# Graph-attention layers with the sources on the partitions and seven groups of destination blocks

## The chip, the cores and the metric

One core of one Trainium2 chip runs the whole program. The metric is the device time of one execution in microseconds. The kernel before took 3711.85 us (median of three runs, 3707.11 to 3715.58).

## The reference

The input is a graph of 3125 nodes with 256 features, 100,000 directed edges and a loop at each node (103,125 edges). Four stages follow, each added to its own input after a layer norm: graph attention with 8 heads of 32 channels, a feed-forward with 16 experts of which each row uses 2, three single-head attention layers with gelu, and a feed-forward on the rows that a router picks. The change is about the third stage, and what prepares it:

```python
def gat_conv(x, src, dst, W, a_src, a_dst, b):
    h = x @ W
    s = h @ a_src
    d = h @ a_dst
    alpha = jax.nn.leaky_relu(s[src] + d[dst], NEG_SLOPE)
    m = jax.ops.segment_max(alpha, dst, num_segments=n)
    ex = jnp.exp(alpha - m[dst])
    denom = jax.ops.segment_sum(ex, dst, num_segments=n)
    w = ex / (denom[dst] + 1e-16)
    out = jax.ops.segment_sum(h[src] * w[:, None], dst, num_segments=n)
    return out + b
x = jax.nn.gelu(gat_conv(x, src, dst, W1, as1, ad1, b1), approximate=False)
```

It is applied three times with other weights; the heads stage is the same with 8 heads and without gelu.

## The kernel before

The edges become a dense matrix `mask_dram` of 3125 x 3200 floats: minus the logarithm of the number of edges, or a large number where there is none. Attention is then dense: for each destination, over all 3125 sources. Nodes stand in 25 blocks of 128 (the last has 53).

The program is a row of phases: edges and nodes to 84 us, the matrix to 450, the heads to 1834, routed nodes and experts to 2308, node projections to 2366, the three layers to 3517, the last feed-forward to 3707. Every engine has its own hand-written list of instructions; waits on semaphores are all that orders one against another.

**Heads** (`heads_phase`). Two passes of four heads over 25 blocks, 200 units in all; a unit is one head of one block, destinations on the partitions. DVE computes the 3125 scores (L977), adds the mask and takes the minimum of the negated scores (`maxima`, L981). ACT exponentiates in two halves (`exps`, L914) and sums as it goes. PE transposes the probabilities in four groups of 7, 6, 6 and 6 tiles into two banks `psT` (L1013), ACT copies each to SBUF (`copy_out`, L923), and PE multiplies (L1027) into one of three banks `psO`. Once a block ACT copies the sums (`copy_sums`, L929), PE turns them (L1034) and ACT writes the rows in four scaled pieces (`rows`, L938). POOL adds the two halves of the denominators (L886) and stores the rows; SP loads the masks, 1568 KB a block.

**Projections** (`node_project_phase`) make for each node the features times W with two more columns, and spread one of them over all partitions as `el` in two versions (times 1 and times the slope).

**Layers** (`layers_phase`). The same scheme as in the heads with one head of 256 channels and 25 blocks a layer:

- DVE: `maxima` (L1308, L1312, L1316) two blocks ahead; `sums` and `rows` (L1342 to L1361); the copies of what the next layer needs: `copy_x` (L1368), `copy_h` (L1373), `copy_el` (L1380, L1381).
- ACT: `exps` (L1486), `copy_out` (L1495), `gelu` (L1500), between which its function table is loaded again.
- PE: `transposes` of the probabilities (L1535), `products` (L1546), then for the next layer `transpose_x` (L1556), `project` (L1565) and `spread_el` (L1573).
- SP: one mask load a block (L1287).

A layer can't start before the last block of the one before is projected and spread; `first_maxima` makes the first block's maxima in two parts for that reason (L1326, L1330). In the last layer DVE also adds the stage's input, normalises and sums for the router, and PE turns the result back (L1582, copied at L1421).

## Time and profile before

| | |
|---|---|
| median of three runs | 3711.85 us |
| profiled execution, its own time | 3708.9 us |
| span of its trace | 3707.2 us |
| granted TensorE clock, mean | 0.973 |
| PE, DVE, ACT, POOL busy | 3419.1, 2806.4, 2514.1, 317.8 us |
| HBM read, written | 327.87, 61.11 MB |

The span is one profiled execution from its first to its last instruction; 1.7 us lie around it. A busy time is the sum of an engine's instructions in it. PE is TensorE's matmuls and PEld its weight loads, which run beside them; DVE is VectorE, ACT ScalarE, POOL GpSimd, SP SyncE. In the records a transpose counts once and a product twice. The mean of the busy shares hides that the stages have different limits.

### The profile page before, as it was taken

How to read it: one execution, taken by the hardware profiler on the slowest of the kernel's cores; microseconds unless marked ns; L12 is line 12 of the kernel's file. 1: busy time of each engine (PE TensorE's matmuls, PEld its weight loads, DVE VectorE, ACT ScalarE, POOL GpSimd, SP SyncE). 2: the span in 40 equal slices, each digit the busy share in tenths (PEclk: the TensorE clock that was granted, in tenths of full speed). 3: DMA queues.
4: the chain of work that ended last, by engine and by line, in shares of the span. 5: the costliest groups of instructions: out<-in, count | busy, mean ns of one | idle time of the engine just before them, and what ended most of it. 6: DMA issues, size and time to landing. Idle time of an engine off the chain costs nothing. (4 is left out here: it accounts for less than half of the span.)

```text
span 3707.2 us, 69969 instructions
## 1 busy us (share of the span) xinstructions
PE 3419.1 (92%) x27369; PEld 2683.0 (72%) x27370; DVE 2806.4 (76%) x4237; ACT 2514.1 (68%) x4068; POOL 317.8 (9%) x280
## 2 busy tenths in 40 slices
PE   6999889999999999999769998799999999999999
PEld 4665566666666666666568998688878888888777
DVE  6999999999999999999762222666655565677594
ACT  4999899999999999999711111466656665676532
POOL 1000011001000010010004444000000000000000
PEclk8999999999999999999859999899999999999999
DMA  4433312122124121121158885422223221433101
GB/s 144 173 109 140 130 57 74 56 63 67 56 69 190 56 74 56 63 66 56 51 180 269 234 242 121 142 105 105 105 86 115 105 105 62 175 115 112 37 15 35
DMA packets 144871, 390.36 MB, mean 105 GB/s; under 512 B 20048, under 2 KB 91550, under 8 KB 126750
## 3 DMA queue, kind: packets, MB, share of 16 engines
q1 hardware_dynamic: 120520, 346.56, 26.7%
q0 software_dynamic: 20816, 36.07, 5.0%
q8 instruction: 224, 3.67, 0.4%
q10 hardware_dynamic: 3206, 3.20, 0.4%
q14 instruction: 105, 0.86, 0.1%
HBM read 327.87 MB, written 61.11 MB: 105 GB/s over the span
## 5 line engine op out<-in xcount | busy, mean ns | idle before, releaser
L923 ACT ACTIVATE hd_probsT<-hd_psT 128x768 f32<-128x768 f32 (+1 forms) x800 | 659.9, 852 | 70.5 <-PE hd_psT L1013 70.5
L1027 PE MATMUL hd_psO<-hd_probsT,hx 128*32 128x128 f32 (+1 forms) x10000 | 571.8, 281 | 129.1 <-ACT hd_probsT L923 129.0
L1546 PE MATMUL ly_psO<-hx_a,ly_probsT 128*128 128x256 f32 x2500 | 584.1, 381 | 0.0
L1027 PEld LDWEIGHTS hd_psO<-hd_probsT,hx 128*32 128x32 f32 (+1 forms) x10000 | 317.3, 108 | 322.5 <-ACT hd_probsT L923 216.0
L1495 ACT ACTIVATE ly_probsT<-ly_psT 128x768 f32<-128x768 f32 (+1 forms) x300 | 248.4, 828 | 392.7 <-PE ly_psT L1535 392.5
L1546 PEld LDWEIGHTS ly_psO<-hx_a,ly_probsT 128*128 128x128 f32 x2500 | 454.1, 190 | 71.4 <-issue 16.6
L1013 PE MATMUL hd_psT<-ident,hd_scores 128*128 128x128 f32 (+1 forms) x3325 | 479.0, 281 | 0.0
L977 DVE SCALAR_TENSOR_TENSOR hd_scores<-el_heads,hx 128x3125 f32<-128x3125 f32 x133 | 460.8, 3465 | 0.0
L981 DVE CUSTOM_DVE_ANT_0 hd_scores<-hd_scores,mask_heads 128x3125 f32<-128x3125 f32 x133 | 453.6, 3411 | 5.7
L914 ACT ACTIVATE hd_scores<-hd_scores,negmax 128x1664 f32<-128x1664 f32 (+1 forms) x266 | 429.9, 1616 | 5.6 <-DVE negmax L981 5.6
L1013 PEld LDWEIGHTS hd_psT<-ident,hd_scores 128*128 128x128 f32 (+1 forms) x3325 | 355.6, 141 | 98.9 <-issue 98.9
L1546 PE MATMUL ly_psO<-hx_b,ly_probsT 128*128 128x256 f32 x1250 | 292.0, 381 | 0.0
L488 DVE TENSOR_SCALAR onehot_c<-iotaC,stage_c 128x392 bf16<-128x392 f16 x1176 | 291.5, 326 | 0.0
L1535 PE MATMUL ly_psT<-ident,ly_scores 128*128 128x128 f32 x1875 | 258.0, 276 | 16.6 <-ACT ly_scores L1486 16.6
L2007 ACT ACTIVATE moe_hidden<-moe_ps_h 128x512 f32<-128x512 f32 x64 | 38.2, 597 | 327.1 <-PE moe_ps_h L1972 327.1
L1486 ACT ACTIVATE ly_scores<-ly_scores,ly_negmax 128x1664 f32<-128x1664 f32 (+1 forms) x150 | 239.3, 1595 | 20.7 <-DVE ly_negmax L1312 10.0
L1546 PEld LDWEIGHTS ly_psO<-hx_b,ly_probsT 128*128 128x128 f32 x1250 | 226.9, 189 | 35.6 <-issue 8.3
L1013 PE MATMUL hd_psT<-ident,scores 128*128 128x128 f32 (+1 forms) x1675 | 243.1, 283 | 9.0 <-ACT scores L914 9.0
L1312 DVE CUSTOM_DVE_ANT_0 ly_scores<-ly_scores,ly_mask 128x3125 f32<-128x3125 f32 x73 | 248.9, 3410 | 3.1
L1535 PEld LDWEIGHTS ly_psT<-ident,ly_scores 128*128 128x128 f32 x1875 | 220.9, 142 | 40.4 <-ACT ly_scores L1486 17.1
L1972 PEld LDWEIGHTS moe_ps_h<-moe_xT,moe_w 128*128 128x128 f32 x2048 | 241.5, 194 | 5.5 <-DVE moe_xT L2013 2.2
L1972 PE MATMUL moe_ps_h<-moe_xT,moe_w 128*128 128x128 f32 x2048 | 242.0, 277 | 1.6 <-DVE moe_xT L2013 1.6
(348 smaller groups left out, 5041.0 us busy)
## 6 DMA issues: line engine op xcount, KB each, us to landing
ly_mask<-mask_dram SPq DMA_DIRECT2D x72, 1568.0 KB, 6.6
moe_w<-in_L_ffn_w SPq DMA_DIRECT2D x144, 512.0 KB, 5.0
mask_heads<-mask_dram SPq DMA_DIRECT2D x46, 1568.0 KB, 6.7
mask_dram<-el_heads SPq DMA_DIRECT2D x196, 196.0 KB, 1.9
el_heads<-el_dram SPq DMA_DIRECT2D x5, 1568.0 KB, 9.7
el_heads<-el_slope_dram SPq DMA_DIRECT2D x5, 1568.0 KB, 13.1
x<-x SPq DMA_DIRECT2D x8, 640.0 KB, 8.4
el_heads<-el_dram POOLq DMA_DIRECT2D x3, 1568.0 KB
```

The lines of the kernel that those rows point to most:

```text
L488: last = nc.vector.tensor_scalar(oc[:, k, :], g["iotaC"][:, :], c[:, k:k + 1], None, ALU.is_equal)
L914: nc.scalar.activation(sc[u % 3][:, halves[j]], sc[u % 3][:, halves[j]], ACT.Exp, scale=-1.0, bias=nm[:, u % 3:u % 3 + 1], accum_out=den[: ...
L923: nc.scalar.activation(pT[:, gi % 2, 0:w], psT[gi % 2][:, 0:w], ACT.Copy).then_inc(s_ev, 1)
L977: nc.vector.scalar_tensor_tensor(sc[c][:, :], el[:, h, 0, 0:N], hx[:, b, o:o + 1], el[:, h, 1, 0:N], ALU.subtract, ALU.min).then_inc(s_lk, 1)
L981: nc.vector.tensor_tensor_reduce(out=sc[c][:, :], in0=sc[c][:, :], in1=mask[:, B % 2, 0:N], scale=1.0, scalar=3.0e38, op0=ALU.add, op1=ALU ...
L1013: last = nc.tensor.transpose(psT[gi % 2][0:r, t * P:(t + 1) * P], sc[u % 3][:, c0:c0 + r], g["ident"][:, :])
L1027: last = nc.tensor.matmul(psO[B % 3][cg * CH:(cg + 1) * CH, h * P:(h + 1) * P], hx[0:r, tt, c0:c0 + CH], pT[0:r, gi % 2, t * P:(t + 1) * P ...
L1312: nc.vector.tensor_tensor_reduce(out=sc[:, c, :], in0=sc[:, c, :], in1=mask[:, B % 2, 0:N], scale=1.0, scalar=3.0e38, op0=ALU.add, op1=ALU ...
L1495: nc.scalar.activation(pT[:, gi % 2, 0:w], psT[gi % 2][:, 0:w], ACT.Copy).then_inc(s_ev, 1)
L1535: last = nc.tensor.transpose(psT[gi % 2][0:r, t * P:(t + 1) * P], sc[:, B % 3, c0:c0 + r], g["ident"][:, :])
L1546: last = nc.tensor.matmul(psO[B % 2][:, 0:D], pT[0:r, gi % 2, t * P:(t + 1) * P], hx[B // NB % 2][0:r, tt, 0:D], start=tt == 0, stop=tt == ...
L1972: last = nc.tensor.matmul(out[:, m * P:(m + 1) * P], w12[:, t % WS, i, k, m * P:(m + 1) * P], xT[:, t % 2, k, :], start=k == 0, stop=k == 1)
```

## The change

The three layers are turned round: sources stand on the partitions and destinations in the free dimension, so that DVE's scores are already the left operand of the product, and no transposes of probabilities or copies of them are left.

- Destination blocks go in seven groups of 3, 3, 4, 5, 5, 3 and 2. A group has 13 steps of two source tiles; scores, exponentials and mask pieces stand in a ring of four steps. Each block of a group has a PSUM bank of its own, with 257 columns: column 0 of the table is ones, so its product is the denominator.
- The scores need each destination's shift along the free dimension. DVE makes the maxima as before (custom operation of 3125 columns, without the score operation ahead of it) for the blocks of the next group, at the steps named in `at_step`, computes two numbers a destination from them (`shifts`), PE spreads these over the partitions (`spread_rows`) and ACT copies them (`copy_rows`).
- The sums of a group are copied out of PSUM one block at a time by ACT (`drain`) after the exponentials of the next group's step 1; `rows` on DVE and `gelus` on ACT follow at step 3.
- `copy_x`, `copy_h` and `copy_el` go from DVE to ACT; the last layer's additions go to POOL, its normalisation to ACT.
- The next layer's first three maxima are made in three pieces of 2560, 384 and 181 columns and joined (`maxima_part`, `maxima_joined`); those of layer 0 in four pieces in the projection phase, which loads three masks now.
- The turned mask `maskT_dram` is made in the heads: PE transposes 3 or 4 tiles of the block's mask a unit into a bank of its own (`turn_mask`, `psM`; `psO` has two banks then), ACT copies them (`copy_mask`) and SP stores them (`store_turned`). The router phase writes the changed diagonal into both matrices.
- In the heads ACT copies the rows in one piece, and POOL multiplies them by the reciprocals.

The core of the diff (left out: the declarations, the projection phase, the pieces of the maxima, the last layer's own operations and the loops of SP and POOL):

```diff
-        psO = [ctx.enter_context(nc.psum_tensor(f"hd_psO{i}", [P, 512], F32)) for i in range(3)]
+        psO = [ctx.enter_context(nc.psum_tensor(f"hd_psO{i}", [P, 512], F32)) for i in range(2)]
+        psM = ctx.enter_context(nc.psum_tensor("hd_psM", [P, 512], F32))
+        mt = sb("mask_turned", [P, 2, HG * P])
...
+            def store_turned(j):
+                b, r, ks = j // HG % NB, dest(j), chunk(j)
+                sp.wait_ge(s_mc, j + 1)
+                whole = [k for k in ks if k < FULL]
+                sp.dma_start(g["maskT_dram"][whole[0] * P:(whole[-1] + 1) * P, b * P:b * P + r].rearrange("(k p) d -> p k d", p=P),
+                             mt[:, j % 2, 0:len(whole) * P].rearrange("p (k d) -> p k d", d=P)[:, :, 0:r]).then_inc(s_mst[j % 2], 16)
...
                 if B + 1 < BLOCKS:
                     halves_added(B + 1)
+                pool.wait_ge(s_raw, B + 1)
+                pool.wait_ge(s_rd, B + 1)
+                rows_ = y[:, B % 3, :].rearrange("p (h c) -> p h c", c=CH)
+                nc.gpsimd.tensor_tensor(rows_, rows_, rden[:, B % 3, :].rearrange("p (h o) -> p h o", o=1).broadcast_to([P, HG, CH]),
+                                        ALU.mult).then_inc(s_y, 1)
...
                     act.wait_ge(s_store[i], 16 * (B // 3))
-                for h in range(HG):
-                    last = nc.scalar.activation(y[:, i, h * CH:(h + 1) * CH], psY[:, h * CH:(h + 1) * CH], ACT.Copy,
-                                                scale=rden[:, i, h:h + 1])
-                last.then_inc(s_y, 1)
+                nc.scalar.activation(y[:, i, :], psY[:, 0:P], ACT.Copy).then_inc(s_raw, 1)
+            def copy_mask(j):
+                act.wait_ge(s_mT, j + 1)
+                if j >= 2:
+                    act.wait_ge(s_mst[j % 2], stored_upto(j - 2))
+                w = len(chunk(j)) * P
+                nc.scalar.activation(mt[:, j % 2, 0:w], psM[:, 0:w], ACT.Copy).then_inc(s_mc, 1)
...
+                    if gi == 3 and u + 2 < UNITS:
+                        copy_mask(u + 2)
...
+            def turn_mask(j):
+                B = j // HG
+                r = dest(j)
+                if B >= 2:
+                    pe.wait_ge(s_mask[B % 2], 16 * (B // 2))
+                if j:
+                    pe.wait_ge(s_mc, j)
+                for t, k in enumerate(chunk(j)):
+                    m = min(P, N - k * P)
+                    last = nc.tensor.transpose(psM[0:m, t * P:t * P + r], mask[0:r, B % 2, k * P:k * P + m], g["ident"][0:r, 0:r])
+                last.then_inc(s_mT, 1)
...
+SIZES = (3, 3, 4, 5, 5, 3, 2)
...
+KC = 2
+NCK = -(-NB // KC)
+RING = 4
...
+        at_step = {5: (0, 1, 2, 3, 5), 4: (0, 1, 3, 5), 3: (0, 2, 4), 2: (1, 3)}
+        first_steps = (2, 4, 6)
+        assert SIZES[1] == len(first_steps)
+        shift_step = lambda G: 7 if G % NG == 1 else 5
...
+        turn_at = {}
+        for gi in range(NG - 1):
+            for i in range(SIZES[gi]):
+                turn_at[STARTS[gi] + i] = (gi + 1) * NCK + 4 + (i if gi + 1 == NG - 1 else 2 * i)
...
+            def load_turned(C):
+                G, c = C // NCK, C % NCK
+                c0, w, s = STARTS[G % NG] * P, width(G), C % RING
+                if C >= RING:
+                    sp.wait_ge(s_msk, C - RING + 1)
+                ks = tiles(c)
+                r = depth(ks[-1])
+                sp.dma_start(mT[0:r, s, 0:len(ks), 0:w],
+                             g["maskT_dram"][ks[0] * P:ks[0] * P + len(ks) * r, c0:c0 + w].rearrange("(k p) d -> p k d", p=r)).then_inc(s_mT[s], 16)
...
+                    nc.gpsimd.tensor_tensor(x[:, b, :], x[:, b, :], y_last[:, b, :], ALU.add).then_inc(s_add, 1)
...
+            def scores(C):
+                G, c = C // NCK, C % NCK
+                l, w, s = G // NG, width(G), C % RING
+                if C >= RING:
+                    multiplied(dve, C - RING)
...
+                for i, k in enumerate(tiles(c)):
+                    r = depth(k)
+                    last = nc.vector.scalar_tensor_tensor(pb[0:r, s, i, 0:w], rw[0:r, G % 2, 0, 0:w], hx[l % 2][0:r, k, N8:N8 + 1],
+                                                          rw[0:r, G % 2, 1, 0:w], ALU.add, ALU.min)
+                last.then_inc(s_lk, 1)
+            def masked(C):
+                G, c = C // NCK, C % NCK
+                w, s = width(G), C % RING
+                n, r = len(tiles(c)), depth(tiles(c)[-1])
+                dve.wait_ge(s_lk, C + 1)
+                dve.wait_ge(s_mT[s], 16 * (C // RING) + 16)
+                nc.vector.tensor_tensor(pb[0:r, s, 0:n, 0:w], pb[0:r, s, 0:n, 0:w], mT[0:r, s, 0:n, 0:w], ALU.add).then_inc(s_msk, 1)
...
+                nc.vector.tensor_tensor_reduce(out=m[:, 0:N], in0=el[B // NB % 2][:, 0:N], in1=m[:, 0:N], scale=1.0, scalar=3.0e38,
+                                               op0=ALU.add, op1=ALU.min, accum_out=q[:, G % 2, d:d + 1]).then_inc(s_nm, 1)
...
+            def rows(G):
+                l, n = G // NG, size(G)
+                dve.wait_ge(s_dr, first_of(G) + n)
...
+                for gi in range(NG):
+                    G = G0 + gi
+                    for c in range(NCK):
+                        C = G * NCK + c
+                        scores(C)
+                        if gi or c:
+                            masked(C - 1)
+                        if gi + 1 < NG:
+                            for d in range(size(G + 1)):
+                                if maxima_at[first_of(G + 1) + d] == C:
+                                    maxima(first_of(G + 1) + d, G + 1)
+                            if c == shift_step(G + 1):
+                                shifts(G + 1)
+                        elif l < LAST and c in (4, 6, 8):
+                            maxima_part(l + 1, 0, (c - 4) // 2)
+                        if gi and c == 3:
+                            rows(G - 1)
+                        if l == LAST and gi:
...
+            def exps(C):
+                G, c = C // NCK, C % NCK
+                l, w, s = G // NG, width(G), C % RING
+                act.wait_ge(s_msk, C + 1)
+                for i, k in enumerate(tiles(c)):
+                    r = depth(k)
+                    last = nc.scalar.activation(pb[0:r, s, i, 0:w], pb[0:r, s, i, 0:w], ACT.Exp, scale=-1.0,
+                                                bias=hx[l % 2][0:r, k, B2:B2 + 1])
+                last.then_inc(s_ex, 1)
...
+            def drain(G):
+                if G:
+                    done = first_of(G)
+                    act.wait_ge(s_y, done)
+                    if (G - 1) // NG < LAST:
+                        act.wait_ge(s_xT, done)
+                for d in range(size(G)):
+                    act.wait_ge(s_done, first_of(G) + d + 1)
+                    nc.scalar.activation(ob[:, d, :], psO[d][:, 0:D + 1], ACT.Copy).then_inc(s_dr, 1)
...
+                    for c in range(NCK):
+                        t = gi * NCK + c
+                        exps(G * NCK + c)
+                        if gi and c == 1:
+                            drain(G - 1)
+                        if gi and c == 3:
+                            gelus(G - 1)
+                        if gi + 1 < NG and c - shift_step(G + 1) in range(1, 1 + 2 * SPREADS[gi + 1], 2):
+                            copy_rows(G + 1, (c - shift_step(G + 1)) // 2)
+                        if l < LAST:
+                            for b in due(t - 1):
+                                copy_x(l * NB + b)
...
+            def products(C):
+                G, c = C // NCK, C % NCK
+                l, w, s = G // NG, width(G), C % RING
+                pe.wait_ge(s_ex, C + 1)
+                for i, k in enumerate(tiles(c)):
+                    r = depth(k)
+                    for d in range(size(G)):
+                        if k == 0 and G and d < size(G - 1):
+                            pe.wait_ge(s_dr, first_of(G - 1) + d + 1)
+                        m = min(P, w - d * P)
+                        last = nc.tensor.matmul(psO[d][0:m, 0:D + 1], pb[0:r, s, i, d * P:d * P + m], hx[l % 2][0:r, k, 0:D + 1],
+                                                start=k == 0, stop=k == NB - 1)
+                        if k == NB - 1:
+                            last.then_inc(s_done, 1)
+                if c < NCK - 1:
+                    last.then_inc(s_mm, 1)
...
+                    for c in range(NCK):
+                        t = gi * NCK + c
+                        products(G * NCK + c)
+                        if gi + 1 < NG and c - shift_step(G + 1) in range(0, 2 * SPREADS[gi + 1], 2):
+                            spread_rows(G + 1, (c - shift_step(G + 1)) // 2)
+                        if l < LAST:
+                            for b in due(t - 1):
+                                project(l * NB + b)
+                            for b in due(t):
+                                transpose_x(l * NB + b)
+                            for b in due(t - 2):
+                                spread_el(l * NB + b)
```

How the rows of each engine move. First ACT in the heads, around the write of a block's rows (`hd_y_stage`); `scores` and `hd_scores` are the three score buffers. Before:

```order
L923 ACTIVATE hd_probsT<-hd_psT 128x768
L938 ACTIVATE hd_y_stage<-hd_psY,hd_rden 128x32 x4
L923 ACTIVATE hd_probsT<-hd_psT 128x768
L914 ACTIVATE hd_scores,hd_den<-hd_scores,negmax 128x1461
L923 ACTIVATE hd_probsT<-hd_psT 128x896
L923 ACTIVATE hd_probsT<-hd_psT 128x768
L914 ACTIVATE scores,hd_den<-scores,negmax 128x1664
```

And now:

```order
L959 ACTIVATE hd_probsT<-hd_psT 128x768
L972 ACTIVATE hd_y_stage<-hd_psY 128x128
L959 ACTIVATE hd_probsT<-hd_psT 128x768
L979 ACTIVATE hd_mask_turned<-hd_psM 128x384
L950 ACTIVATE hd_scores,hd_den<-hd_scores,negmax 128x1461
L959 ACTIVATE hd_probsT<-hd_psT 128x896
L959 ACTIVATE hd_probsT<-hd_psT 128x768
L950 ACTIVATE hd_scores,hd_den<-hd_scores,negmax 128x1664
```

The four writes of 32 columns are one of 128, and a copy of the turned mask stands ahead of the second half of the exponentials of the next unit.

Second DVE in the layers. Before, a steady block:

```order
L1308 SCALAR_TENSOR_TENSOR ly_scores<-el,hx_a 128x3125
L1311 MEMSET ly_spare 1x1
L1312 ISA ly_scores,ly_negmax<-ly_scores,ly_mask 128x3125
L1312 ISA ly_negmax 128x1
L1316 TENSOR_SCALAR ly_has_edge<-ly_negmax 128x1
L1380 COPY x<-ly_psX 128x128
L1381 TENSOR_SCALAR x<-ly_psX 128x128
L1368 COPY ly_xT<-ly_psX 128x256
L1342 TENSOR_TENSOR ly_rden<-ly_den 128x1
L1344 RECIPROCAL ly_rden<-ly_rden 128x1
```

Now, from the last step of group 0 to the start of group 1 (three blocks each; L1493 are the scores, L1503 the mask, L1510 a maximum for group 2):

```order
L1493 SCALAR_TENSOR_TENSOR ly_probs<-ly_rows,hx_a 128x384 x2
L1503 TENSOR_TENSOR ly_probs<-ly_probs,ly_mask_turned 53x384
L1510 ISA ly_mask,least<-el,ly_mask 128x3125
L1510 ISA least 128x1
L1493 SCALAR_TENSOR_TENSOR ly_probs<-ly_rows,hx_a 128x384 x2
L1503 TENSOR_TENSOR ly_probs<-ly_probs,ly_mask_turned 128x2x384
L1510 ISA ly_mask,least<-el,ly_mask 128x3125
L1510 ISA least 128x1
L1493 SCALAR_TENSOR_TENSOR ly_probs<-ly_rows,hx_a 128x384 x2
L1503 TENSOR_TENSOR ly_probs<-ly_probs,ly_mask_turned 128x2x384
L1493 SCALAR_TENSOR_TENSOR ly_probs<-ly_rows,hx_a 128x384 x2
L1503 TENSOR_TENSOR ly_probs<-ly_probs,ly_mask_turned 128x2x384
```

One pair of long operations a block has become 13 steps of scores and mask a group, with the maxima of the next group between the first of them.

Third ACT at the same place (L1638 exponentials, L1650 the drain of group 0, L1656 its gelu):

```order
L1638 ACTIVATE ly_probs<-ly_probs,hx_a 53x384
L1638 ACTIVATE ly_probs<-ly_probs,hx_a 128x384 x4
L1650 ACTIVATE ly_sums<-ly_psO 128x257 x3
L1638 ACTIVATE ly_probs<-ly_probs,hx_a 128x384 x4
L1656 ACT_TABLE_LOAD
L1656 ACTIVATE ly_sums<-ly_sums 128x256 x3
L1638 ACT_TABLE_LOAD
L1638 ACTIVATE ly_probs<-ly_probs,hx_a 128x384 x4
```

The drain stands behind the exponentials of steps 0 and 1 of the new group, and the gelu behind those of steps 2 and 3. Before, no such drain existed: DVE read the sums from PSUM at L1361.

## Rows read from the trace of the kernel before

**Rows 1.** Busy us by stretch: PE, PEld, DVE, ACT, POOL; clock, DMA share, GB/s.
```profile
450.00:1834.00 1384.00, 1245.97 (x15400) 893.80 (x15400) 1359.74 (x849) 1298.71 (x1855) 129.42 (x105) 1.00 0.22 70
2366.00:3517.00 1151.00, 1124.32 (x6075) 959.82 (x6075) 712.68 (x1099) 711.02 (x835) 0.00 (x0) 0.99 0.29 104
```

**Rows 2.** Costliest groups, shapes apart, 2366 to 3517 us: busy, mean ns | idle before.
```profile
L1546 PE MATMUL ly_psO<-hx_a,ly_probsT 128*128 128x256 f32 x2400 | 552.8, 379 | 0.0
...
L1312 DVE CUSTOM_DVE_ANT_0 ly_scores<-ly_scores,ly_mask 128x3125 f32<-128x3125 f32 x73 | 248.9, 3410 | 3.1
...
L1308 DVE SCALAR_TENSOR_TENSOR ly_scores<-el,hx_a 128x3125 f32<-128x3125 f32 x49 | 169.8, 3465 | 3.9 <-DMA ly_mask<-mask_dram 2.2 <-PEq L59 1.7
L1486 ACT ACTIVATE ly_scores<-ly_scores,ly_negmax 128x1664 f32<-128x1664 f32 x75 | 125.7, 1676 | 19.9 <-DVE ly_negmax L1312 10.0 <-DVE ly_negmax L1335 9.9
...
L1486 ACT ACT_TABLE_LOAD x76 | 97.5, 1283 | 2.1 <-PEq L59 0.8
```

**Rows 3.** Timeline of a steady block of a layer, PE alone: start us, length us.
```profile
2600.45 0.38 PE L1556 MATMUL ly_psX<-ident,ly_y 128*128 128x128 f32 x2
...
2600.67 0.93 PE L1535 MATMUL ly_psT<-ident,ly_scores 128*128 128x128 f32 x7
...
2601.43 2.95 PE L1546 MATMUL ly_psO<-hx_a,ly_probsT 128*128 128x256 f32 x12
...
2604.31 1.14 PE L1565 MATMUL ly_psH<-wx,ly_xT 128*128 128x258 f32 x4
...
2605.94 3.19 PE L1546 MATMUL ly_psO<-hx_a,ly_probsT 128*128 128x256 f32 x14
...
2608.97 0.27 PE L1573 MATMUL ly_psX<-ident,hx_b 128*128 128x128 f32 x1
```

**Rows 4.** Timeline: first products of layers 0 and 1, first record after the last.
```profile
2377.82 1.59 PE L1546 MATMUL ly_psO<-hx_a,ly_probsT 128*128 128x256 f32 x3
...
2767.88 2.42 PE L1546 MATMUL ly_psO<-hx_b,ly_probsT 128*128 128x256 f32 x7
...
3507.43 0.44 PE L1582 MATMUL ly_psH<-ident,hx_b 128*128 128x128 f32 x2
```

**Rows 5.** Timeline of the boundary between layers 0 and 1.
```profile
2758.06 0.29 DVE L1380 COPY x<-ly_psX 128x128 f32<-128x128 f32 x1 [0.58 <-PE ly_psX L1573]
2758.27 0.28 DVE L1381 TENSOR_SCALAR x<-ly_psX 128x128 f32<-128x128 f32 x1
...
2762.20 0.41 DVE L1326 SCALAR_TENSOR_TENSOR ly_scores<-x,hx_b 128x181 f32<-128x181 f32 x1
...
2765.05 3.04 PE L1535 MATMUL ly_psT<-ident,ly_scores 128*128 128x128 f32 x13 [3.28 <-ACT ly_scores L1486]
```

**Rows 6.** Timeline of the heads: maxima of two units, two copies.
```profile
998.91 3.41 DVE L981 CUSTOM_DVE_ANT_0 hd_scores<-hd_scores,mask_heads 128x3125 f32<-128x3125 f32 x1
...
1004.08 1.50 ACT L923 ACTIVATE hd_probsT<-hd_psT 128x768 f32<-128x768 f32 x2
...
1005.76 3.41 DVE L981 CUSTOM_DVE_ANT_0 scores<-scores,mask_heads 128x3125 f32<-128x3125 f32 x1
```

**Rows 7.** Waits in the heads, 500 to 1800 us: total us, times, longest.
```profile
PE hd_psO L1027 <- ACT hd_probsT L923: 122.6, 238, 1.7
...
ACT hd_probsT L923 <- PE hd_psT L1013: 64.9, 141, 0.7
```

**Rows 8.** Costliest groups of the heads, shapes apart, 500 to 1800 us.
```profile
L923 ACT ACTIVATE hd_probsT<-hd_psT 128x768 f32<-128x768 f32 x568 | 454.6, 823 | 64.9 <-PE hd_psT L1013 64.9
...
L938 ACT ACTIVATE hd_y_stage<-hd_psY,hd_rden 128x32 f32<-128x32 f32 x188 | 38.6, 300 | 0.0
...
L929 ACT ACTIVATE hd_sumsT<-hd_psO 128x512 f32<-128x512 f32 x47 | 27.6, 587 | 0.0
```

**Rows 9.** The tile of the denominators in the heads: least, median and longest ns.
```profile
L886 POOL TENSOR_TENSOR hd_rden<-hd_den x50: 191/1710/3443, 478.5 to 1824.4; 128x4 f32<-128x4 f32 x50
```

**Rows 10.** The page's DMA issues: KB each, us from issue to landing.
```profile
ly_mask<-mask_dram SPq DMA_DIRECT2D x72, 1568.0 KB, 6.6
```

More of the change, by code:

```diff
@@ new lines, in layers_phase @@
+        depth = lambda k: min(P, N - k * P)
+        spreads_upto = lambda G: G // NG * sum(SPREADS) + sum(SPREADS[:G % NG])
+        place, user, landed = {}, {}, {}
+        latest, loads = [None] * len(masks), [0] * len(masks)
+        for B in range(LAYERS * NB):
+            if B < 2:
+                s = B
+            elif B % NB == SIZES[0] - 1:
+                s = 2
+            else:
+                s = 0 if latest[1] > latest[0] else 1
+            place[B], user[B] = s, latest[s]
+            latest[s] = B
+            loads[s] += 0 if B < SIZES[0] else 1
+            landed[B] = loads[s]
@@ L1349, in rows @@
[L1349 to L1362 removed]
+            c_ = Chain(dve, s_c)
@@ L1538, in products @@
[L1538 to L1548 removed]
+            spread = {"rows": 0, "el": 0}
@@ L1550, in transpose_x @@
             def transpose_x(B):
+                b = B % NB
+                gi = max(i for i in range(NG) if STARTS[i] <= b)
                 pe.wait_ge(s_g, B + 1)
```

746 lines of the change are left out of this document (403 added, 343 removed).

## Prediction

> **What bounds the kernel now.** I read the busy times by stage first. The heads take 1384 us with VectorE (DVE) busy for 1360 of them and ScalarE (ACT) for 1299 [rows 1]; the three single-head layers take 1151 us with TensorE (PE) busy for 1124 and DVE and ACT for some 712 each [rows 1]. So DVE sets the heads, with ACT 5% behind it, and PE sets the layers. Next come the costliest groups of the layers [rows 2]: besides the products PE spends its time on transposes of the probabilities. The timeline of a steady block gives PE's cost per tile as the distance between starts: two transposes 0.22 us, seven 0.76 (0.109 each), seven products of 256 columns (14 records) 3.03, so 0.433 each, and a projection 0.98 between its start and that of the next record (its row says 1.14, ends are modelled; I take 0.98) [rows 3]. A block is then 25 x 0.433 + 25 x 0.109 + 1.5 for transpose, projection and spread = 15.05 us, and 25 of them give 376; between the first products of layers 0 and 1 lie 390.1 us, and from the first product of all to the end of the last 1129.6 [rows 4]. The rest, some 14 us, is the boundary between layers.
>
> **Layers: what goes.** With sources on the partitions the probabilities come out of DVE as PE wants them. 25 x 25 x 0.109 = 68 us of transposes a layer leave PE, and ACT's copies of them and most of the table loads (76 at this line alone [rows 2]) go too. That would be 3 x 68 = 204 us if nothing else bound.
>
> **Layers: what comes.** DVE now writes every score twice (add and min, then mask) and also makes the maxima. Its price per column is (3465 - 410) / (3125 - 181) = 1.04 ns [rows 2, 5], and its fixed part is 0.07 us from start to start: two independent operations of 128 columns start 0.21 apart [rows 5]. Per layer: 2 x 25 x 3125 columns = 163 us; 175 score and 91 mask operations x 0.07 = 19; 25 maxima x 3.42 = 86 [rows 2]; rows, shifts 15. Sum 283. PE: 625 products of 257 columns x 0.435 = 271; 25 x 1.5 projections = 38; 50 row spreads x 0.109 = 5. Sum 314. Were the two to run beside each other, a layer would take about 314 + boundary.
>
> They don't quite. The ring holds 4 steps of two tiles, so DVE starts group G when PE has 2.5 steps of group G-1 left, and PE can start G only after DVE has written steps 0 to 2 and masked 0 and 1, with the maxima of the next group in between at steps 0 and 1, ACT has made the exponentials of step 1 and drained the sums (the drain stands behind them on ACT). For three blocks a step's scores are 2 x (0.07 + 0.40) = 0.94, its mask 0.87; so 3 x 0.94 + 2 x 0.87 + 0.45 (last mask of G-1) + 2 x 3.42 = 11.8, exponentials of 384 columns and the first drain 1.7 (1664 columns cost 1.68, I scale and add 0.2 each) [rows 2], in all 13.5. PE has 2.5 x 6 x 0.433 = 6.5. **Idle 7 us** at group 1; with four and five blocks 15.0 against 6.5 and 16.8 against 8.7, so 8.5 and 8; group 4 has one maximum less, 13.3 against 10.8, 2.5. Groups 5 and 6 have none. Behind the later maxima DVE is 3.4 late and PE has a step or two (2.6 to 4.3 us each) in hand: in group 0 each of three maxima stands two steps from the next, and DVE gains 0.8 a step on PE's 2.6, so 3.4 - 1.6 = 1.8 shows each time, and 2.5 at the start; I allow further 3 in each of groups 1 to 3, 2 in each of the rest: 8 + 9 + 6 = 23. The boundary is a chain as now, drain, rows, gelu, transpose, copy, project, spread, last piece of the maxima, and now also join, shifts, spread of the rows and their copies before the first scores: about 17, of which 2 are in PE's sum. Total 314 + 26 + 23 + 15 = 378, I take **376** against 390 now. The last layer has no projections and no boundary, but turns back (25 x 0.22), and DVE makes sums and statistics, some 25 x 0.9, of which I put a third on the path: 376 - 15 - 38 + 6 + 8 = 337. First product to last: 2 x 376 + 337 = 1089 for 1129.6, **-40**. Bounds: if every maximum's 3.42 beyond the second of a group came through to PE, 12 x 3.4 = 40 more per layer (+120, nothing left); if the alternation hid itself, 49 less per layer (-147).
>
> **Other terms.** Maxima of the first blocks in the projection phase: three blocks wait for the last piece only, against 3.5 + 3.4 us of scores and maxima now; but join, shifts, spread and copies come in, and three bias and router loads stand ahead of the first mask tile on SP: +2.5 (0 to 5). Router phase: an element-wise transfer more, beside DVE work that ends later: +1 (0 to 6). Mask traffic doubles to 78 MB a layer, from a DMA share of 0.29 [rows 1] to some 0.6. A slot of the ring is filled again three steps ahead, 7.8 us at PE's pace for three blocks; its 393 KB behind a whole mask (1568 KB land in 6.6 us [rows 10]) are there after 6.6 x 1.25 = 8.3, so 0.5 late where both meet: 0 to +25 in all, I take nothing, since PE's slack covers it.
>
> **The heads.** ACT gets a copy of 384 columns from PSUM a unit. 512 columns take 0.587 [rows 8]; a copy of 768 takes 0.82 [rows 8], two of them 1.50, so 0.68 from start to start [rows 6]; 384 columns are then 0.36 to 0.47. One row copy for four saves about 3 x 0.17 a block (each 0.30 long [rows 8], some 0.13 of it behind the next start), 0.13 a unit. Net +0.24 to +0.34 a unit, 48 to 68 us in 200 units; I take 52, nearer the lower end, since ACT's queue is seldom empty. Its cover is what it waits now: 64.9 for the transposes over 190 units, 0.34 a unit [rows 7], of a unit of 6.85 us (from one maximum to the next [rows 6]). PE gets 3 transposes, 0.33, against 122.6 / 190 = 0.65 of waiting [rows 7]. On totals it fits. But these waits are those of a ring of two banks between PE and ACT, in which an added piece of either delays the other, and a late exponential frees a score buffer late for DVE. The new copy stands ahead of the second half of the exponentials, on that path. I put a third of the 52 on DVE's path: **+17** (0 to +68). POOL now multiplies 128x128 from SBUF once a block. Its 128x4 operation takes 191 ns at least, 1710 in the median and 3443 at most [rows 9], one DVE operation: it waits for one to end. The Trainium skill, "SBUF — State Buffer", section "SBUF: two separate sides", calls the pair of ports an exclusive lock that blocks the other side for a whole instruction; the rows agree for POOL, and none shows DVE blocked; by that rule DVE would lose POOL's whole operation and this term would be +14. DVE's operation stays at 3465 in the mean beside it. If POOL holds DVE up, it is for some 0.29 us, as long as DVE's own copy of 128 columns [rows 5], 14 in 50 blocks; I take a third, **+5** (0 to +14), since DVE issues first nearly always. In the last layer POOL makes 50 additions of 256 columns the same way: **+6** (0 to +15). The store's 39 MB beside a DMA share of 0.22 [rows 1]: nothing.
>
> **Sum.** -40 + 2.5 + 1 + 17 + 5 + 6 = -8.5 on the profiled execution's 3708.9 (3 below the median): 3700.4, I write 3700.
>
> **Rivals.**
> (a) *The heads become ACT's.* All of the net addition comes through, +52, in place of +17: 3735. It decides from where ACT's unit with the copy passes 6.85, as its 0.34 of waiting is for PE, which is loaded itself. For it: ACT at 1299 of 1384. Against: the waits exceed the addition. With the layers at +15 worse, 3750. Chance 0.22.
> (b) *The layers alternate more than I reckon*, as every wait on the ring of 4 adds a hop: 15 us more a layer, 3745, or the whole 120 of the bound, 3820. Chance 0.10.
> (c) *They alternate less*: DVE catches up while PE drains, idle only 10 to 15 a layer, of 49, -100: 3600. Chance 0.09.
> (d) *The heads hide all and POOL costs nothing*: 3675. Chance 0.17.
> (e) *DVE operations don't overlap.* Each would cost its whole length, 0.22 + 1.04 ns per column by the row of 181 columns at 0.41 [rows 5], 0.15 more, times 266 is 40 us a layer; DVE at 323 passes PE: +90, 3790. The two starts 0.21 apart with a length of 0.29 speak against it. The Trainium skill, "VectorE: DVE Perf Modes", section "The DRAIN you can't avoid", has this rule: the next operation does not start until the pipe is empty. The trace does not bear it out. Chance 0.03.
> (f) *PE's clock falls in the idle of each group.* After a pause 13 transposes took 3.04 [rows 5], twice 13 x 0.109. Some 1.5 us after each of 12 gaps: +18, 3718. Chance 0.05.
>
> The forecast as worked out has 0.34.
>
> **How the numbers follow.** 0.2%, 7.4 us, is about what a measurement can tell. The forecast lies just past that on the fast side: 0.21 of its 0.34 faster, 0.10 same, 0.03 slower. With (c) and (d) faster is 0.47; (f) and what is close to it make same 0.16; (a), (b), (e) make slower 0.37. The range reaches to most of (a) and (b) above and past (d) below: 3642 to 3762.
>
> **What would show it.** In the profile after: DVE and PE busy shares in the layers near 283/376 and 314/376; PE waiting for ACT's exponentials of step 0 or the drain some 7 us at groups 1 to 3, with the maxima ahead of it on DVE; 376 between first products. Heads 1384 to 1410 long, ACT waits for the mask's transposes small, DVE waiting for exponentials where it never waited. Wrong would be: heads unchanged and layers at 350 (then c and d); DVE idle in the heads over 40 us (a); DVE operations beside POOL longer than 3.47 (the lock); scores operations of 384 columns starting over 0.5 apart (e).

## The result

The changed kernel takes 3762.47 us (median of four runs, 3756.59 to 3766.93), the kernel before 3713.72 beside it (four runs, 3707.11 to 3718.16): 1.0137 times as long, 95% interval 1.0125 to 1.0149. 3700 had been forecast, with 3642 to 3762 as the range and faster the likeliest. It is slower by 49 us.

The page of the changed kernel (its head, the row of the granted clock and of DMA in 40 slices, and the costliest groups that answer to [rows 2] and [rows 5]; columns as there):

```profile
span 3765.2 us, 69232 instructions
...
PE 3381.5 (90%) x26419; PEld 2610.6 (69%) x26420; DVE 3024.6 (80%) x4442; ACT 2371.5 (63%) x4270; POOL 427.1 (11%) x382
...
PEclk8999999999999999999869998899998999989999
DMA  5433332232344323233277885576547663775201
...
L1760 PE MATMUL ly_psO<-hx_a,ly_probs 128*128 128x257 f32 (+2 forms) x2500 | 610.2, 399 | 105.6 <-ACT ly_sums L1650 66.9
...
L1024 DVE CUSTOM_DVE_ANT_0 hd_scores<-hd_scores,mask_heads 128x3125 f32<-128x3125 f32 x133 | 459.7, 3456 | 5.7
...
L1638 ACT ACTIVATE ly_probs<-ly_probs,hx_a 128x384 f32<-128x384 f32 (+5 forms) x350 | 213.4, 660 | 235.0 <-DVE ly_probs L1503 234.8
...
L1493 DVE SCALAR_TENSOR_TENSOR ly_probs<-ly_rows,hx_a 128x384 f32<-128x384 f32 (+5 forms) x350 | 228.7, 693 | 122.1 <-PE ly_psO L1760 97.1
...
L1503 DVE TENSOR_TENSOR ly_probs<-ly_probs,ly_mask_turned 128x768 f32<-128x768 f32 (+7 forms) x273 | 287.1, 1052 | 3.6 <-DMA ly_mask_turned<-mask_turned_dram 3.6
```

PE has less to do than before (3381 for 3419 us) and DVE more (3025 for 2806), as forecast. But the products now have idle time before them, and the digits of the clock fall again and again in the last third. The stretches (columns as in [rows 1]): the heads, then each layer from its first product to the next one's:

```profile
450.00:1834.00 1384.00, 1302.95 (x15916) 955.59 (x15917) 1368.01 (x848) 1339.43 (x1896) 170.47 (x150) 1.00 0.32 98
2404.00:2801.00 397.00, 347.94 (x1550) 281.18 (x1550) 295.96 (x398) 166.65 (x329) 0.00 (x0) 0.93 0.61 205
2801.00:3194.00 393.00, 346.12 (x1551) 280.57 (x1552) 296.85 (x400) 166.92 (x330) 0.00 (x0) 0.93 0.60 200
3194.00:3567.00 373.00, 317.88 (x1383) 254.10 (x1384) 314.86 (x472) 175.05 (x307) 63.28 (x46) 0.92 0.59 194
```

Before, PE was busy for 98% of the layers at a clock of 0.99 [rows 1]. Now it is busy for 347 us of 397 at 0.93. The two profiled executions, by the starts of the same operations in the traces, differ like this:

| stretch | before | after | difference | forecast |
|---|---|---|---|---|
| to the last write of a row in the heads | 1832.3 | 1844.3 | +12.0 | +17 and +5 |
| from there to the first product of the experts | 106.2 | 107.7 | +1.5 | +1 |
| products of the experts | 360.9 | 369.8 | +8.9 | 0 |
| to the first product of the layers | 78.4 | 82.0 | +3.6 | +2.5 |
| first to last product of the layers | 1129.3 | 1162.8 | +33.5 | -40 and +6 |
| from there to the end | 200.1 | 198.6 | -1.5 | 0 |

That is 58 us between the spans. The experts' code is the same in both; in the profiles of the changed kernel and its ten variants their products took 362.9 to 374.8 us, and in the one profile of the kernel before 360.9. The phase varies by more than 10 us from one profile to another; whether it is also longer on the average after the change stays open. The medians lie 49 us apart, 9 less than these two executions. The surprise is the layers: 67 us off.

In the heads DVE's maxima have another longest length (least, median and longest ns, to be set against 3410 throughout before):

```profile
L1024 DVE CUSTOM_DVE_ANT_0 hd_scores<-hd_scores,mask_heads x133: 3409/3410/3639, 455.9 to 1825.5; 128x3125 f32<-128x3125 f32 x133
```

Of the 199 that the two names of the buffers have together, 36 take about 3.64 us and 12 about 3.49, in all 9 us more than 3.41 each: three quarters of the heads' 12. ACT's wait for PE fell from 64.9 us [rows 7] to 35.2 in the same stretch:

```profile
ACT hd_probsT L959 <- PE hd_psT L1056: 35.2, 140, 1.6
```

ACT is busy for 41 us more in the heads (1339 for 1299), and most of that came out of this wait.

In the layers, the start of group 1 of layer 1 (timeline; PE's idle time before it in brackets):

```profile
2848.48 0.91 ACT L1650 ACTIVATE ly_sums<-ly_psO 128x257 f32<-128x257 f32 x3
...
2848.99 12.80 PE L1760 MATMUL ly_psO<-hx_b,ly_probs 128*128 128x257 f32 x48 [7.53 <-ACT ly_sums L1650]
2849.27 3.40 DVE L1510 CUSTOM_DVE_ANT_0 ly_mask<-x,ly_mask 128x3125 f32<-128x3125 f32 x1
```

PE stands still for 7.5 us and starts when the first sums are drained, behind step 1. At groups 1 to 3 of layers 0 and 1 these gaps are 7.5 us each, at group 4 it is 2.2, where 7, 8.5, 8 and 2.5 had been worked out; groups 5 and 6, which were to have none, have 1.8 and 1.5. Then 48 records of products take 12.80 us, where 48 x 0.2165 [rows 3] are 10.4: the first ten take twice their time. The granted clock there is 0.5 (1.2 of 2.4 GHz), from 6 us before the first of them until 4.4 after it.

### The profile page after: what moved, and what is told of

The parts are those of the page before. It is cut to its first block and busy times, and to the rows that moved or that the text cites. A ratio compares the mean times of both kernels' runs of the same rounds, so it can differ in the third digit from the quotient of the medians.

```text
span 3765.2 us, 69232 instructions
## 1 busy us (share of the span) xinstructions
PE 3381.5 (90%) x26419; PEld 2610.6 (69%) x26420; DVE 3024.6 (80%) x4442; ACT 2371.5 (63%) x4270; POOL 427.1 (11%) x382
## 5 line engine op out<-in xcount | busy, mean ns | idle before, releaser
L1760 PE MATMUL ly_psO<-hx_a,ly_probs 128*128 128x257 f32 (+2 forms) x2500 | 610.2, 399 | 105.6 <-ACT ly_sums L1650 66.9
L1760 PEld LDWEIGHTS ly_psO<-hx_a,ly_probs 128*128 128x128 f32 (+2 forms) x2500 | 475.0, 196 | 220.6 <-ACT ly_probs L1638 119.9
L1638 ACT ACTIVATE ly_probs<-ly_probs,hx_a 128x384 f32<-128x384 f32 (+5 forms) x350 | 213.4, 660 | 235.0 <-DVE ly_probs L1503 234.8
L1760 PE MATMUL ly_psO<-hx_b,ly_probs 128*128 128x257 f32 (+2 forms) x1250 | 302.9, 396 | 40.2 <-ACT ly_sums L1650 27.9
L1493 DVE SCALAR_TENSOR_TENSOR ly_probs<-ly_rows,hx_a 128x384 f32<-128x384 f32 (+5 forms) x350 | 228.7, 693 | 122.1 <-PE ly_psO L1760 97.1
L1760 PEld LDWEIGHTS ly_psO<-hx_b,ly_probs 128*128 128x128 f32 (+2 forms) x1250 | 235.9, 194 | 94.7 <-ACT ly_probs L1638 45.4
L1503 DVE TENSOR_TENSOR ly_probs<-ly_probs,ly_mask_turned 128x768 f32<-128x768 f32 (+7 forms) x273 | 287.1, 1052 | 3.6 <-DMA ly_mask_turned<-mask_turned_dram 3.6
L549 PE MATMUL cnt<-onehot_c,onehot_dst_a 128*128 128x392 bf16 x1176 | 232.9, 335 | 8.9 <-DVE onehot_c L488 8.6
L1024 DVE CUSTOM_DVE_ANT_0 scores<-scores,mask_heads 128x3125 f32<-128x3125 f32 x66 | 228.0, 3455 | 2.8
```

Source lines behind the costliest of these rows:

```text
L549: last = nc.tensor.matmul(o, ohA[:, s, :, k], ohC[:, s, k, :], start=k == 0 and not further, stop=True, skip_group_check=True)
L1024: nc.vector.tensor_tensor_reduce(out=sc[c][:, :], in0=sc[c][:, :], in1=mask[:, B % 2, 0:N], scale=1.0, scalar=3.0e38, op0=ALU.add, op1=ALU ...
L1493: last = nc.vector.scalar_tensor_tensor(pb[0:r, s, i, 0:w], rw[0:r, G % 2, 0, 0:w], hx[l % 2][0:r, k, N8:N8 + 1], rw[0:r, G % 2, 1, 0:w], ...
L1503: nc.vector.tensor_tensor(pb[0:r, s, 0:n, 0:w], pb[0:r, s, 0:n, 0:w], mT[0:r, s, 0:n, 0:w], ALU.add).then_inc(s_msk, 1)
L1760: last = nc.tensor.matmul(psO[d][0:m, 0:D + 1], pb[0:r, s, i, d * P:d * P + m], hx[l % 2][0:r, k, 0:D + 1], start=k == 0, stop=k == NB - 1)
```

## The experiments

Times are medians, to be compared with 3762.5 unless said otherwise; the kernel before took 3711.3, 3713.2 and 3710.0 us beside the three sets.

Four theories. **A**: PE's gaps at the start of groups, with the half clock behind them, and the narrow last block. **B**: the doubled mask traffic stalls DVE. **C**: DVE's sum is the bound, in whatever order. **D** came after the first set: a cycle between DVE and PE that the ring closes.

**Drain first.**

```diff
-                        if gi and c == 1:
+                        if gi and c == 0:
                             drain(G - 1)
```

> The changed kernel, with the drain of a group's sums on ACT after the exponentials of step 0 of the next group instead of step 1. Theory A (the layers lose by alternation: PE stands idle at the start of groups 1 to 3 until the drain behind step 1, 7.5 us each, and runs at half clock after it): the first product comes up to 5.7 us earlier, step 1 comes when it came, so a step of PE's work (2.6 to 4.3 us) moves into the idle time of groups 1 to 3 and some 2.4 us in groups 4 and 5, 13 to 15 us a layer, in all 35 to 45 us less than the changed kernel, about 3722. Theory B (the doubled mask traffic is what stalls DVE): nothing, 3760. Theory C (DVE is the bound of the layers, since its operations cost more than I reckoned): nothing or under 10 us.

3758.5 us, 4 less. PE's records at the start of group 1 of layer 1, with the waits of step 0, of step 1 and of step 3:

```profile
2833.00 4.52 PE L1760 MATMUL ly_psO<-hx_b,ly_probs 128*128 128x257 f32 x12 [2.26 <-ACT ly_sums L1650]
...
2837.90 5.47 PE L1760 MATMUL ly_psO<-hx_b,ly_probs 128*128 128x257 f32 x24 [0.38 <-ACT ly_probs L1638]
...
2846.68 3.68 PE L1760 MATMUL ly_psO<-hx_b,ly_probs 128*128 128x257 f32 x8 [3.32 <-ACT ly_probs L1638]
```

The gap before the first product has shrunk (2.3 us instead of 7.5), and the time has not: one of 0.4 came before step 1 and one of 3.3 before step 3, and the layer takes 392 us as before. In the whole layer PE's waits are 44 us instead of 47. The mean granted clock of the layer rose from 0.93 to 0.95, but what its products take beyond their length at the full clock only fell from 13 us to 12. The gap that I had put at the head of the list was slack of another chain, and theory A falls as to its main term.

**Wide last block.**

```diff
-                        m = min(P, w - d * P)
+                        m = P
```

> The changed kernel, with the last block's products 128 wide like the others (its 53 destinations and 75 columns of older numbers, whose sums nobody reads). In the trace of the changed kernel a product pair of the last group takes 1.20 us (128 wide, then 53 wide, with PE's weight loads idle 0.33 to 0.40 before each), against 0.87 for two of 128. Theory A with this as one of its terms: 0.33 x 25 tiles x 3 layers = 25 us less, about 3737. Theories B and C: DVE and DMA keep their work, so under 5 us.

3740.3 us, 22 less, as expected. The rows of the changed kernel that it rests on (timeline, last group of layer 0):

```profile
2745.42 2.44 PE L1760 MATMUL ly_psO<-hx_a,ly_probs 128*128 128x257 f32 x8 [1.45 <-ACT ly_sums L1650]
...
2748.77 2.36 PE L1760 MATMUL ly_psO<-hx_a,ly_probs 128*128 128x257 f32 x8
```

Eight records, four products, take 2.36 us, 1.18 for a pair instead of 0.87. PE's weight loads at the same place stand idle before each change of width:

```profile
2749.30 0.17 PEld L1760 LDWEIGHTS ly_psO<-hx_a,ly_probs 128*53 128x53 f32 x2 [0.33 <-issue]
2749.86 0.30 PEld L1760 LDWEIGHTS ly_psO<-hx_a,ly_probs 128*128 128x128 f32 x2 [0.40 <-issue]
```

**Maxima later.**

```diff
-        at_step = {5: (0, 1, 2, 3, 5), 4: (0, 1, 3, 5), 3: (0, 2, 4), 2: (1, 3)}
+        at_step = {5: (2, 3, 4, 5, 6), 4: (2, 4, 5, 7), 3: (2, 4, 6), 2: (2, 4)}
-        shift_step = lambda G: 7 if G % NG == 1 else 5
+        shift_step = lambda G: 6 if size(G) == 5 else 7
```

> The changed kernel, with the maxima for the next group at steps 2 and later (2,3,4,5,6 for five; 2,4,5,7 for four; 2,4,6 for three; 2,4 for two) and the shifts at step 6 or 7. Theory A: no maximum stands ahead of the first two steps, so the idle 7.5 us at the start of groups 1 to 3 go to nearly nothing, and with them most of the half clock there; part comes back as waits behind the crowded maxima: 40 to 60 us less, about 3710. Theory B: nothing. Theory C (DVE's sum is the bound, whatever its order): nothing.

3784.6 us, 22 more, where 40 to 60 less had been expected. The wait of DVE's scores for the copied rows of the new group, in the changed kernel and then here (2400 to 3500 us: total, times, longest):

```profile
DVE ly_probs L1493 <- ACT ly_rows L1663: 24.4, 9, 3.4
...
DVE ly_mask L1510 <- DMA ly_mask<-mask_dram: 6.8, 2, 3.9
...
DVE ly_probs L1503 <- DMA ly_mask_turned<-mask_turned_dram: 3.6, 2, 2.9
```

```profile
DVE ly_probs L1493 <- ACT ly_rows L1663: 78.7, 15, 10.3
```

With the shifts later the rows are spread later, at steps up to 10, and DVE may not begin a group before them. The gaps before the first products of groups 1 to 3 did shrink, to 2 to 4 us in layers 0 and 1; that did not help, as it had not with the drain first.

**The mask stays.** The turned pieces are loaded for the first four steps only.

```diff
             def load_turned(C):
+                if C >= RING:
+                    return
```

> The changed kernel, but the pieces of the turned mask are loaded once, into the four slots of the ring, and never again (39 MB a layer less; the masks for the maxima are loaded as ever). It leaves out the right mask from the fifth step on. Theory A: DVE waited 10 us in all for DMA in the layers, so 5 to 12 us less, about 3753. Theory B: the layers lose their excess, 40 to 75 us less, 3690 to 3720. Theory C: as A.

3762.9 us, no difference. The kernel reads 115 MB less from HBM (38 a layer; the DMA share of layer 1 falls from 0.60 to 0.29) and the time is the same, so theory B is out. Nor did the 5 to 12 us come that A and C expected: even the 6.8 and 3.6 us of waits for DMA in the fence above cost nothing that shows.

**Rows scaled on ACT in the heads**, as before the change:

```diff
-                nc.scalar.activation(y[:, i, :], psY[:, 0:P], ACT.Copy).then_inc(s_raw, 1)
+                for h in range(HG):
+                    last = nc.scalar.activation(y[:, i, h * CH:(h + 1) * CH], psY[:, h * CH:(h + 1) * CH], ACT.Copy,
+                                                scale=rden[:, i, h:h + 1])
```

> The changed kernel, with the rows of the heads scaled by ACT in four pieces as before the change, and without POOL's multiplication (the turned masks are still made, copied and stored). Lock theory (POOL's operation with its two inputs from SBUF holds DVE up by 0.23 us once a block, the longest of DVE's maxima being 3.64 us where it was 3.41): all maxima take 3.41 again and the heads end 9 to 10 us earlier, 3750. Its rival (ACT is now the bound of the heads, and its copies of the turned mask are what costs the 10 us): ACT gets some 25 us more work, so the heads end as late or later, 3762 to 3785.

3788.3 us, 26 more, just beyond the rival's range. Each theory was right in a part:

```profile
L1023 DVE CUSTOM_DVE_ANT_0 hd_scores<-hd_scores,mask_heads x133: 3409/3410/3414, 456.8 to 1847.5; 128x3125 f32<-128x3125 f32 x133
```

```profile
DVE hd_scores L1019 <- PE hd_psT L1055: 14.5, 30, 0.6
...
DVE scores L1019 <- PE hd_psT L1055: 7.3, 16, 0.5
```

No maximum is longer than 3.414 us any more, so it was POOL's multiplication that held DVE up. But DVE now waits for PE in the loop with ACT (21.8 us here, 1.3 in the changed kernel): the heads end 24 us later. The changed kernel's heads stand at the edge of rival (a), and the multiplication on POOL, at 9 us, is what keeps them off it.

**Last layer's additions on DVE.**

```diff
-                nc.gpsimd.tensor_tensor(x[:, b, :], x[:, b, :], y_last[:, b, :], ALU.add)
+                nc.vector.tensor_tensor(x[:, b, :], x[:, b, :], y_last[:, b, :], ALU.add)
```

> The changed kernel, with the additions of the last layer on DVE (50 of 256 columns, 0.34 each from start to start) and none on POOL. Lock theory: DVE's small operations beside POOL's go back to their length (the shifts took 0.6 there for 0.16 in the layers before), which gives back some 20 us of DVE, and the additions cost 17, of which a part is on the path: 5 to 15 us less, 3747 to 3757. Rival (the last layer is long for its statistics alone): DVE gets 17 us more work and nothing back, 5 to 17 us more, 3767 to 3780.

3758.6 us, 4 less. An operation of 5 columns or fewer in the changed kernel and then here (least, median, longest ns):

```profile
L1536 DVE SCALAR_TENSOR_TENSOR ly_top<-ly_top x21: 160/163/649, 2391.5 to 3503.7; 128x3 f32<-128x3 f32 x9, 128x5 f32<-128x5 f32 x6, 128x4 f32<-128x4 f32 x3, 128x2 f32<-128x2 f32 x3
```

```profile
L1518 DVE SCALAR_TENSOR_TENSOR ly_top<-ly_top x21: 160/163/166, 2386.2 to 3493.4; 128x3 f32<-128x3 f32 x9, 128x5 f32<-128x5 f32 x6, 128x4 f32<-128x4 f32 x3, 128x2 f32<-128x2 f32 x3
```

The longest falls from 649 to 166. In the last layer DVE is busy for 314.4 us with the additions, and was for 314.9 without them: POOL's 50 additions had cost DVE about as much as making them costs it. The 4 us lie just below what the lock theory expected, and are no more than such runs differ by.

**Rings of four and of six.** Six slots of 640 columns don't fit in SBUF beside the rest; with groups of at most four blocks they do. The diff is that of the run with six; the one with four has RING = 4. Both also have the drain first and the wide last block, so they differ in RING alone.

```diff
-SIZES = (3, 3, 4, 5, 5, 3, 2)
+SIZES = (3, 3, 4, 4, 4, 4, 3)
-RING = 4
+RING = 6
+MASK_RING = 4
...
-in range(0, 2 * SPREADS[gi + 1], 2):
+in range(0, SPREADS[gi + 1]):
```

> The changed kernel, with groups of 3, 3, 4, 4, 4, 4 and 3, the rows spread in successive steps, the drain after step 0 and the last block's products 128 wide; the ring still has four steps. Theory D (DVE and PE alternate in a cycle: DVE may begin a group when PE has done step 9 of the one before, and the maxima that come then end in PE's own time only as far as the ring reaches): with the ring at four the cycle stays, and there are the 22 us of the wide last block, some 15 of the more even groups and few of the rest, 3720 to 3730. Theory C (the sum of DVE's work is the bound, whatever the ring): 3735 to 3740, the wide block alone.

> As the run before with groups of 3, 3, 4, 4, 4, 4 and 3, but with a ring of six steps for the scores (the pieces of the mask still have four). Theory D: DVE may begin a group two steps (5 to 7 us) earlier in PE's time, so most of its maxima fall beside PE's products; 50 to 65 us less than with four steps, 3660 to 3680. Theory C: no more than 5 us less than with four steps. Theory B (DMA): nothing, since the loads are the same.

3736.6 us with four and 3674.3 with six: 62 us for two more slots, nothing else changed. The run with four is not where theory D had it (3720 to 3730) but where C had (3735 to 3740): it is only 4 us below the wide last block alone, so the 15 us for the more even groups did not come. The run with six is where D had it, and C had allowed 5 us less. It is 0.9896 times the kernel before (0.9875 to 0.9918). Layer 1 with four, then layers 0 to 2 with six (columns as in [rows 1]):

```profile
2783.00:3166.00 383.00, 338.73 (x1550) 284.17 (x1550) 295.52 (x399) 166.92 (x329) 0.00 (x0) 0.95 0.61 206
```

```profile
2401.00:2762.00 361.00, 332.40 (x1551) 282.33 (x1552) 294.35 (x399) 166.78 (x329) 0.00 (x0) 0.96 0.67 226
2762.00:3116.00 354.00, 330.70 (x1550) 281.04 (x1549) 292.97 (x398) 166.28 (x328) 0.00 (x0) 0.97 0.66 221
3116.00:3471.00 355.00, 308.65 (x1379) 257.47 (x1380) 312.32 (x468) 173.23 (x302) 84.65 (x44) 0.96 0.63 205
```

With the same operations DVE is busy for 296 us of 383 with four slots, and for 293 of 354 with six. DVE's waits for a slot (the second row) and ACT's for DVE in that layer, with four and then with six, show where it went:

```profile
ACT ly_probs L1639 <- DVE ly_probs L1504: 93.8, 39, 6.5
DVE ly_probs L1494 <- PE ly_psO L1761: 65.2, 36, 3.0
```

```profile
ACT ly_probs L1639 <- DVE ly_probs L1504: 59.8, 26, 6.1
...
DVE ly_probs L1494 <- PE ly_psO L1761: 22.6, 10, 3.7
```

PE's own waits between records fall from 44 to 24 us, and the records at double length from 42 to 20. Theory C is out, and theory D stands as to what the ring does; what it said of four slots did not come.

**Ring of six, spread and drain as in the change.** The same without the two smaller edits:

> The version with groups of 3, 3, 4, 4, 4, 4 and 3, a ring of six and the wide last block, but with the rows spread at every second step and the drain after step 1, as the change has them. Theory D (the ring is what frees DVE; the drain's place only decides how soon PE gets going again): 3685 to 3700, the drain costing PE some 1 to 2 us a group now that PE is nearly never idle. If the ring works only together with the earlier spread of the rows, since DVE may not begin a group without them: 3720 to 3740.

3681.5 us, 7 more than with them (and 3 below what theory D expected): the ring does nearly all. Group 1 of layers 0 and 1 still begins here after 7.5 us without work, and the kernel is faster than the one before (0.9917, 0.9900 to 0.9933), so that gap was not what made the change lose. Against the wide last block alone this run differs in the ring and in the sizes of the groups, and it is 59 us shorter.

**Ring of six, additions on DVE.**

> The version of 3674 us (ring of six, rows spread in successive steps, drain after step 0), with the last layer's additions on DVE instead of POOL. Lock theory: DVE's operations in the last layer get their length back for 17 us of additions; with the ring of four this gave 4 us, with six, where DVE's own sum weighs more against PE's, 0 to 10 us less, 3664 to 3674. Rival (DVE is short of time there and the additions are simply more): 3676 to 3690.

3671.1 us, 3 less, within what these runs can tell from nothing. It is the shortest of all, 0.9889 times the kernel before (0.9873 to 0.9906).

## Why the prediction was wrong

**The layers.** The step that failed is "Total 314 + 26 + 23 + 15 = 378, I take **376**", and the one for the last layer that is built on it. The sum had PE's waits, and more of them than came. It took all of PE's own work at the full clock, and all products at the price of 128 columns. By the records of the trace the two steps compare as follows with layer 1 (its first product to the next layer's) and layer 2 (to its last product). Products are counted at 0.2165 us a record; double length is what records over 0.6 us took beyond that; waits are gaps between PE's records.

| us | worked out, layer 1 | measured | worked out, layer 2 | measured |
|---|---|---|---|---|
| products | 271 | 271 | 271 | 270 |
| PE's other work | 43 | 51 | 11 | 17 |
| PE waits | 64 | 47 | 57 | 55 |
| products at double length | 0 | 13 | 0 | 17 |
| narrow block | 0 | 7 | 0 | 7 |
| single slower products | 0 | 5 | 0 | 7 |
| sum | 378 | 393 | 339 | 373 |

- The gaps at the starts of groups 1 to 4 were right to 1 us. Two terms were missing. The half clock was rival (f), at 0.05 and 1.5 us after each of 12 gaps, 18 us. In the three layers together the products took 44 us more by it, and with PE's other work in the stretches of a granted clock of 0.5 it is 53. Its place was wrong too: in the layers 194 of 3750 product records are longer than 0.6 us, also after gaps of 1.8 to 2.9 us. No run varies the clock by itself, so this is an account of PE's time and not a saving that a run showed.
- The narrow block stood in no rival: I took 257 columns times the number of products, and [rows 3] showed no pair of widths. It is 21 us in the trace, and 22 came back when it was made wide.
- PE's other work is 8 and 6 us more; a part is the boundary, 19.8 us from the end of the last product to the next layer's first, where 17 was worked out. A part of PE's work in it ran at half clock, as these rows show (eight spreads in 2.08, where 0.87 would do):

```profile
2780.95 0.87 ACT L1650 ACTIVATE ly_sums<-ly_psO 128x257 f32<-128x257 f32 x2 [5.76 <-PE ly_psO L1760]
...
2783.61 0.44 PE L1788 MATMUL ly_psX<-ident,ly_sums 128*128 128x128 f32 x2 [2.21 <-ACT ly_sums L1656]
...
2792.39 2.08 PE L1777 MATMUL ly_psR<-ident,ly_uv 128*128 128x128 f32 x8 [2.37 <-DVE ly_uv L1539]
...
2801.20 2.08 PE L1760 MATMUL ly_psO<-hx_b,ly_probs 128*128 128x257 f32 x4 [4.81 <-ACT ly_probs L1638]
```

- In the last layer "of which I put a third on the path" held for PE's waits, 55 for 57 in all, but the gaps at the group starts grew (to 10.6 us at group 3) and with them the products at double length.
- The price of a DVE operation's fixed part was taken from two copies of 128 columns out of PSUM. Two scores of 384 columns, in group 1 of layer 1, take 1.13 us, and the mask after them starts 1.06 after the first:

```profile
2847.34 1.13 DVE L1493 SCALAR_TENSOR_TENSOR ly_probs<-ly_rows,hx_b 128x384 f32<-128x384 f32 x2
2848.40 0.95 DVE L1503 TENSOR_TENSOR ly_probs<-ly_probs,ly_mask_turned 128x768 f32<-128x768 f32 x1
```

  That is 0.53 from start to start, with 0.61 for the length of one, so the fixed part is 0.13 and not 0.07: DVE is busy for 297 us a layer and not 283. The sign given for rival (e), starts over 0.5 apart, came, and (e) did not: it had the whole 0.61 and DVE above PE, and DVE's 297 stay below PE's 314. The Trainium skill, "VectorE: DVE Perf Modes", section "The DRAIN you can't avoid", says that the next operation waits until the pipe is empty, which would be 0.61 here, and adds that one which is not held starts earlier; the 0.53 agrees with the addition.
- The bounds of the sum were wrong as well. "If every maximum's 3.42 beyond the second of a group came through to PE" and "if the alternation hid itself" enclosed the waits and not the clock, and the range of the whole was cut at 3762 where both could add. (The first also counts 12 such maxima a layer, and groups of 3, 3, 4, 5, 5, 3 and 2 have 11.)

By size this is nearest to rival (b), which had a chance of 0.10 and 15 us more a layer: it was 21, 17 and 36 more. But (b) had PE wait more than worked out, and it waited less (49, 47 and 55 us, for 64, 64 and 57). Two questions have to be kept apart. Why the forecast missed is in the table. Why the change loses was settled by the rings: two more slots take 62 us away, waits and double length together, and the kernel is then faster than the one before. The gaps at the group starts, which the prediction named, don't settle it: such a gap ends in its own time when the drain moves, and the layer takes as long.

**The heads.** +12 for +22 in the two terms, and the shares were wrong: the total is nearer than its parts. The lock was worked out as 0.29 a block or 14 at most, taken at 5 and measured as 9; the sign given for it, DVE operations beside POOL over 3.47, came. The "third of the 52" on ACT was taken at 17, and 3 at most is left for it; the run with rows on ACT shows that it was close to more. The Trainium skill, "SBUF — State Buffer", section "SBUF: two separate sides", has the lock for DVE operations with two inputs from SBUF against POOL's; the maxima are such, and here it shows on both sides: POOL's multiplication takes 0.396 us in the median and up to 3.64 behind a DVE operation. By that rule of a whole instruction a maximum would lose all that is left of POOL's multiplication when it starts, some 0.36 (POOL starts 0.03 ahead of it); it loses 0.23.

**Smaller terms.** The start of the layers +3.6 for +2.5, the router phase +1.5 for +1, DMA 0 for 0. The experts' 9 us were not forecast and are not explained (their code is the same).

## What to carry over

When two engines hand work to each other through a ring of buffers, ask which cycle of waits the ring closes, and how far ahead of the other it lets the engine go that begins first; a gap that the timeline shows may be slack of that cycle, and moving the instruction that ends it moves the gap. Two more slots (62 us) were worth 15 times the reordering (4 us). And price PE's work behind each of its gaps at half clock too when you add up its time; here the sum left out 44 us of it. Closing one gap need not give them back: with the drain first only 5 of the 44 went.

## What the runs showed of the hardware

- A product whose left operand is 53 columns wide, beside one of 128, costs more than another of 128: a pair takes 1.18 us, with weight loads idle 0.33 to 0.40 before each change of width, against 0.87. Making it wide took 22 us off the kernel.
- After gaps of 7.5 us PE ran the next 6 to 13 records of products at a granted clock of 0.5, each in 0.43 us instead of 0.22; after 2.2 and 1.8 us still 6 or 7 of them.
- POOL's operations with two inputs from SBUF lengthen DVE's of the same kind: maxima by 0.23 us, and operations of 5 columns or fewer from 0.16 to as much as 0.65. Both are gone when POOL's operations are.
- With 38 MB a layer of DMA less, a share of 0.29 instead of 0.60, the time was the same.
